# Where the padding mask is added in a cross attention of 1601 keys: TensorE's product or VectorE, tile by tile

## The reference

```python
q = _split_heads(query @ Wq.T + bq)        # 16 heads of 16 channels
k = _split_heads(key @ Wk.T + bk)
v = _split_heads(value @ Wv.T + bv)
scores = jnp.einsum('bhqd,bhkd->bhqk', q, k) / jnp.sqrt(jnp.float32(DEPTH))
scores = scores + mask * jnp.float32(-1000000000.0)
weights = jax.nn.softmax(scores, axis=-1)
ctx = jnp.einsum('bhqk,bhkd->bhqd', weights, v)
```

## Time and profile before

| | |
|---|---|
| median of 3 runs | 2710.78 us |
| lowest, highest | 2704.63, 2714.89 us |
| the profiled execution, its time | 2712.94 us |
| its span, first to last instruction | 2711.2 us |
| mean granted TensorE clock | 0.882 |
| busy: TensorE, VectorE, ScalarE, GpSimd | 2228.2, 1308.1, 956.8, 687.1 us |
| first cross attention, exp of the first to the last tile | 79.2 to 921.4 us (start of the last) |
| second cross attention, scoresT of the first to the last tile | 1439.0 to 2307.5 us |

### The profile page before, as it was taken

How to read it: one execution, slowest core, us unless ns; L and a number is a source line. 1 busy time by engine, 2 the same in 40 slices (tenths; PEclk the granted TensorE clock), 3 DMA queues, 4 the chain that set the end, 5 groups by cost and what they waited for, 6 DMA issues and landing times. The chain is left out here.

```text
span 2711.2 us, 59977 instructions
## 1 busy us (share of the span) xinstructions
PE 2228.2 (82%) x24624; PEld 1817.9 (67%) x24624; DVE 1308.1 (48%) x2900; ACT 956.8 (35%) x1689; POOL 687.1 (25%) x505
## 2 busy tenths in 40 slices
PE   5799999999999732869958999999999999844443
PEld 3677887888888611659946888888888888422223
DVE  3445454554545478231144545454545455344445
ACT  3244444444444232213232444444444444110001
POOL 3121222122121000100043443344434440033320
PEclk9799999999999675969987999999999999765557
DMA  4455555555554100143235555565565653000000
GB/s 116 112 132 127 136 128 138 124 126 136 130 130 105 44 21 0 35 144 109 79 100 131 137 141 140 137 141 139 138 143 141 142 122 79 18 0 0 0 0 22
DMA packets 166860, 267.45 MB, mean 99 GB/s; under 512 B 70713, under 2 KB 86210, under 8 KB 166594
## 3 DMA queue, kind: packets, MB, share of 16 engines
q1 hardware_dynamic: 166594, 263.66, 39.3%
HBM read 98.70 MB, written 1.05 MB: 37 GB/s over the span
## 5 line engine op out<-in xcount | busy, mean ns | idle before, releaser
L691 DVE CUSTOM_DVE_ANT_0 scores_d<-scores_d,mask_scaled_d 128x512 f32<-128x512 f32 (+1 forms) x512 | 281.4, 601 | 145.8 <-PE scores_d L536 142.8
L648 ACT ACTIVATE exp_d<-scoresT_d 128x512 f32<-128x512 f32 (+1 forms) x416 | 248.6, 598 | 274.2 <-PE scoresT_d L570 272.0
L695 DVE TENSOR_REDUCE max_parts_a<-scores_a 128x1 f32<-128x512 f32 (+1 forms) x512 | 263.6, 567 | 152.1 <-PE scores_a L536 152.1
L648 ACT ACTIVATE exp_a<-scoresT_a 128x512 f32<-128x512 f32 (+1 forms) x416 | 248.2, 597 | 210.5 <-PE scoresT_a L570 208.8
L570 PEld LDWEIGHTS scoresT_d<-q_stack_d,k_stack_d 128*128 128x128 f32 (+1 forms) x1664 | 244.8, 187 | 24.1
L570 PE MATMUL scoresT_a<-q_stack_a,k_stack_a 128*128 128x128 f32 (+1 forms) x1664 | 259.4, 281 | 0.9 <-DVE q_stack_a L712 0.9
L570 PEld LDWEIGHTS scoresT_a<-q_stack_a,k_stack_a 128*128 128x128 f32 (+1 forms) x1664 | 230.2, 195 | 28.0 <-issue 3.2
L570 PE MATMUL scoresT_d<-q_stack_d,k_stack_d 128*128 128x128 f32 (+1 forms) x1664 | 228.0, 260 | 0.0
L536 PE MATMUL scores_a<-k_stack_a,q_stack_a 96*128 96x512 f32 (+1 forms) x512 | 175.2, 395 | 42.7 <-DMA k_stack_a<-k_hi_a 20.7
L679 DVE SCALAR_TENSOR_TENSOR k_lo_d<-project_d,bk_d,k_hi_d 128x512 fp32r<-128x512 f32 (+1 forms) x128 | 81.0, 635 | 258.2 <-ACT k_hi_d L631 258.2
L679 DVE SCALAR_TENSOR_TENSOR k_lo_a<-project_a,bk_a,k_hi_a 128x512 fp32r<-128x512 f32 (+1 forms) x128 | 81.0, 635 | 253.5 <-ACT k_hi_a L631 253.4
(11 more groups left out here) (371 smaller groups left out, 4882.6 us busy)
## 6 DMA issues: line engine op xcount, KB each, us to landing
k_stack_a<-k_hi_a SPq DMA_DIRECT2D x256, 128.0 KB
k_stack_d<-k_hi_d SPq DMA_DIRECT2D x256, 128.0 KB
raw_a<-in_ctxT SPq DMA_DIRECT2D x48, 512.0 KB, 4.1
raw_d<-in_ctxT SPq DMA_DIRECT2D x48, 512.0 KB, 4.9
w_c<-in_L_ffn_W SPq DMA_DIRECT2D x23, 1024.0 KB, 8.7
k_stack_a<-k_hi_a SPq DMA_DIRECT2D x256, 72.2 KB, 2.1
k_stack_d<-k_hi_d SPq DMA_DIRECT2D x256, 72.2 KB
k_stack_a<-k_lo_a SPq DMA_DIRECT2D x128, 128.0 KB
```

The source lines that it names most:

```text
L648: nc.scalar.activation(eT[at % RING][0:r, :], ST[at % 2][0:r, :], ACT.Exp).then_inc(exp_done, 1)
L691: nc.vector.tensor_tensor_reduce(SC[at % 3][:, 0:w], SC[at % 3][:, 0:w], mf[m % 2][:, BANK * chunk:BANK * chunk + w], 1.0, NEG, ALU.add, A ...
L695: nc.vector.reduce_max(parts[:, j, chunk:chunk + 1], SC[at % 3][:, 0:w], AX.X).then_inc(score_free, 1)
```

## The change

In tiles 0, 1, 3, 7, 9 and 12 of the second attention scoresT has no mask product. VectorE adds the mask into the PSUM bank instead: scalar_tensor_tensor computes mask x -1e9 + scores over 128 x 512, the mask read from a new tile mT, laid out by keys, and repeated over the 8 heads. exp of these tiles waits for that add. In VectorE's list the add comes first in its slot. mT is a new input, transposed and cut to these six tiles on the host; one DMA a sequence brings it (196 KB), two at the start and then one behind keys(g + 2, 1) in odd iterations, where it waits for the last add of its buffer's former sequence. mb keeps only columns 256 to 1536, so GpSimd's copy and subtraction shrink from 1601 to 1280 columns. own0 goes, its two uses write into rec. The first attention is built from the same functions and keeps its instructions, but for own0.

```diff
--- before.py
+++ after.py
@@ -292,6 +292,8 @@
 S_SLOT = {0: [0], 1: [1], 2: [2, 3], 3: [4], 4: [5, 6], 5: [7], 6: [8, 9], 7: [10], 8: [11, 12], 9: [13], 10: [14, 15]}
 SUM_SLOT = 5
 MAX_SLOT = 11
+ADD_TILES = [0, 1, 3, 7, 9, 12]
+SPLIT_FROM, SPLIT_TO = 2 * P, 12 * P
 GROUPS = HALVES * NB
 
 
@@ -326,7 +328,7 @@
 PROJECTION, SCORE = projections(), score_banks()
 
 
-def cross_attention(nc, chip, cross, qT, attnT, wk, wv, bk, bv, mask, late, late_in, tag):
+def cross_attention(nc, chip, cross, qT, attnT, wk, wv, bk, bv, mask, maskT, late, late_in, tag):
 
     masked = mask is not None
     RING = 3
@@ -347,11 +349,12 @@
         qs = [sb(f"q_stack{i}", [P, PAIRS, P], F32R) for i in range(2)]
         turn, high = sb("neg_max_cols", [P, PW]), sb("neg_max_hi", [P, 4], F32R)
         parts = sb("max_parts", [P, 4, 4])
-        kept, rec, own0 = sb("out_copy", [P, P]), sb("rec", [P, P]), sb("own0", [P, T])
+        kept, rec = sb("out_copy", [P, P]), sb("rec", [P, P])
         if masked:
             mf = [sb(f"mask_scaled{i}", [P, KEYS]) for i in range(2)]
-            mb = [sb(f"mask_hi_lo{i}", [P, KPAD], F32R) for i in range(2)]
+            mb = [sb(f"mask_hi_lo{i}", [P, SPLIT_TO - SPLIT_FROM], F32R) for i in range(2)]
             pick = sb("pick", [P, P], F32R)
+            mT = [sb(f"maskT{i}", [P, len(ADD_TILES), T]) for i in range(2)]
         SC = [ctx.enter_context(nc.psum_tensor(f"scores{i}{tag}", [P, BANK], F32)) for i in range(3)]
         ST = [ctx.enter_context(nc.psum_tensor(f"scoresT{i}{tag}", [P, BANK], F32)) for i in range(2)]
         PJ = [ctx.enter_context(nc.psum_tensor(f"project{i}{tag}", [P, BANK], F32)) for i in range(2)]
@@ -360,6 +363,7 @@
         set_up, q_hi_done, q_split, q_in, q_ready = (
             sem(n) for n in ("set_up", "q_hi_done", "q_split", "q_in", "q_ready"))
         mask_in, mask_step, mask_ready = [sem(f"mask_in{i}") for i in range(2)], sem("mask_step"), sem("mask_ready")
+        maskT_in, mask_added = [sem(f"maskT_in{i}") for i in range(2)], sem("mask_added")
         k_projected, v_projected, k_hi_done = sem("k_projected"), sem("v_projected"), sem("k_hi_done")
         project_free = [sem(f"project_free{i}") for i in range(2)]
         stacked = [sem("stacked_a"), sem("stacked_b")]
@@ -413,8 +417,15 @@
                     sp.dma_start(mf[m % 2][T * k:T * k + T, :],
                                  mask[m:m + 1, :, :].rearrange("a q k -> (a q) k")).then_inc(mask_in[m % 2], 16)
 
+            def masksT(m):
+                if m >= 2:
+                    sp.wait_ge(mask_added, 2 * len(ADD_TILES) * (m - 1))
+                sp.dma_start(mT[m % 2][:, :, :], maskT[m:m + 1, :, :, :].rearrange("a p t q -> p (a t) q")
+                             ).then_inc(maskT_in[m % 2], 16)
+
             if masked:
                 masks(0)
+                masksT(0)
             queries(0)
             cross.load(sp, 1, 0)
             cross.load(sp, 1, 1)
@@ -422,6 +433,7 @@
             keys(0, 1)
             if masked:
                 masks(1)
+                masksT(1)
             queries(1)
             keys(1, 0)
             keys(1, 1)
@@ -438,6 +450,8 @@
                         queries(n + 2)
                 keys(g + 2, 0)
                 keys(g + 2, 1)
+                if masked and h and n + 2 < NB:
+                    masksT(n + 2)
             sp.wait_ge(ctx_ready, 4 * NB)
             for tile, view in late:
                 sp.dma_start(tile, view).then_inc(late_in, 16)
@@ -474,9 +488,9 @@
                 pool.wait_ge(mask_in[m % 2], 32 * (m // 2) + 32)
                 nc.gpsimd.tensor_scalar(raw[:, :], raw[:, :], -1.0e9, None, ALU.mult).then_inc(mask_step, 1)
                 pool.wait_ge(mask_step, 2 * m + 1)
-                nc.gpsimd.tensor_copy(out[:, 0:KEYS], raw[:, :]).then_inc(mask_step, 1)
+                nc.gpsimd.tensor_copy(out[:, :], raw[:, SPLIT_FROM:SPLIT_TO]).then_inc(mask_step, 1)
                 pool.wait_ge(mask_step, 2 * m + 2)
-                nc.gpsimd.tensor_tensor(out[T:P, 0:KEYS], raw[T:P, :], out[T:P, 0:KEYS].bitcast(F32),
+                nc.gpsimd.tensor_tensor(out[T:P, :], raw[T:P, SPLIT_FROM:SPLIT_TO], out[T:P, :].bitcast(F32),
                                         ALU.subtract).then_inc(mask_ready, 1)
                 pool.wait_ge(mask_ready, m + 1)
 
@@ -562,14 +576,15 @@
                     if masked and h == 0:
                         pe.wait_ge(mask_ready, m + 1)
                 after(pe, exp_done, at - 1)
-                if masked:
-                    nc.tensor.matmul(bank[0:r, :], mb[m % 2][:, cols],
+                by_product = masked and t not in ADD_TILES
+                if by_product:
+                    nc.tensor.matmul(bank[0:r, :], mb[m % 2][:, P * t - SPLIT_FROM:P * t - SPLIT_FROM + P],
                                      pick[:, :].rearrange("p (a c) -> p a c", a=1).to_broadcast([P, 4, P]),
                                      start=True, stop=False, skip_group_check=True)
                 for j in range(4):
                     ins = nc.tensor.matmul(bank[0:r, P * j:P * j + P], stack[h][:, j, cols],
-                                           qs[m % 2][:, 4 * h + j, :], start=not masked, stop=True,
-                                           skip_group_check=masked)
+                                           qs[m % 2][:, 4 * h + j, :], start=not by_product, stop=True,
+                                           skip_group_check=by_product)
                 ins.then_inc(scoredT, 1)
 
             def values(g, t):
@@ -643,7 +658,10 @@
 
             def exp(g, t):
                 at, r = KT * g + t, rows(t)
-                act.wait_ge(scoredT, at + 1)
+                if masked and t in ADD_TILES:
+                    act.wait_ge(mask_added, len(ADD_TILES) * g + ADD_TILES.index(t) + 1)
+                else:
+                    act.wait_ge(scoredT, at + 1)
                 after(act, values_done, at - RING + 1)
                 nc.scalar.activation(eT[at % RING][0:r, :], ST[at % 2][0:r, :], ACT.Exp).then_inc(exp_done, 1)
 
@@ -694,6 +712,16 @@
                 else:
                     nc.vector.reduce_max(parts[:, j, chunk:chunk + 1], SC[at % 3][:, 0:w], AX.X).then_inc(score_free, 1)
 
+            def add_mask(g, t):
+
+                at, r, m, i = KT * g + t, rows(t), g // 2, ADD_TILES.index(t)
+                if i == 0 and g % 2 == 0:
+                    dve.wait_ge(maskT_in[m % 2], 16 * (m // 2) + 16)
+                dve.wait_ge(scoredT, at + 1)
+                bank = ST[at % 2][0:r, :].rearrange("p (a q) -> p a q", q=T)
+                nc.vector.scalar_tensor_tensor(bank, mT[m % 2][0:r, i:i + 1, :].to_broadcast([r, BANK // T, T]), -1.0e9,
+                                               bank, ALU.mult, ALU.add).then_inc(mask_added, 1)
+
             def negate(g):
 
                 cols, at = turn[:, 0:16].rearrange("p (j k) -> p j k", k=4), SCORE["max", g]
@@ -724,10 +752,10 @@
                 dve.wait_ge(score_free, at + 1)
                 nc.vector.tensor_tensor(rec[:, :], kept[:, :], rec[:, :], ALU.mult).then_inc(out_step, 1)
                 dve.wait_ge(out_step, 3 * g + 1)
-                nc.vector.tensor_scalar(own0[:, :], rec[:, 0:T], own[:, 0:1], bv[:, h:h + 1], ALU.mult,
+                nc.vector.tensor_scalar(rec[:, 0:T], rec[:, 0:T], own[:, 0:1], bv[:, h:h + 1], ALU.mult,
                                         ALU.add).then_inc(out_step, 1)
                 dve.wait_ge(out_step, 3 * g + 2)
-                nc.vector.scalar_tensor_tensor(attnT[:, h, T * n:T * n + T], rec[:, T:P], own[:, 1:2], own0[:, :],
+                nc.vector.scalar_tensor_tensor(attnT[:, h, T * n:T * n + T], rec[:, T:P], own[:, 1:2], rec[:, 0:T],
                                                ALU.mult, ALU.add).then_inc(out_step, 1)
 
             nc.vector.memset(turn[:, :], 0.0)
@@ -744,6 +772,8 @@
             for g in range(GROUPS):
                 m, h = g // 2, g % 2
                 for t in range(KT):
+                    if masked and t in ADD_TILES:
+                        add_mask(g, t)
                     if t == MAX_SLOT and g + 1 < GROUPS:
                         negate(g + 1)
                         place_max(g + 1)
...
@@ -1874,6 +1904,9 @@
     a = {k: np.asarray(v) for k, v in inputs.items()}
     o = {"x": a["x"].reshape(NT, P, D), "constants": CONSTANTS, "dispatch_tables": TABLES, "ctxT": a["ctx_1024"].transpose(0, 2, 1),
          "mask": a["mask_Bx1xSxS2_fk0"].reshape(NB, T, KEYS)}
+    by_key = np.zeros((NB, KT * P, T), np.float32)
+    by_key[:, :KEYS] = o["mask"].transpose(0, 2, 1)
+    o["maskT"] = by_key.reshape(NB, KT, P, T)[:, ADD_TILES].transpose(0, 2, 1, 3)
     for k, v in a.items():
         if k.startswith(("L0_", "L1_")):
             o[k] = v
```

More of the change, by code:

```diff
@@ L1774, in _, with cross_stage @@
                                                ALU.mult, ALU.add)
-def cross_stage(nc, chip, dram, layer, tag, mask):
+def cross_stage(nc, chip, dram, layer, tag, mask, maskT):
```

(6 more changed lines are left out.)

## The result

| | before | after |
|---|---|---|
| median of 4 runs each (before: the three above and one more) | 2707.70 us | 2749.22 us |
| lowest, highest | 2695.89, 2714.89 | 2740.09, 2757.90 |
| the profiled execution | 2712.94 | 2757.90 |
| second attention, first to last instruction on its tiles | 971.1 | 1005.6 |

The ratio is 1.0157, 95% interval 1.0107 to 1.0208: the change is slower by 1.6%, outside the range forecast. A **drop** is a stretch of a few us in groups 2 to 29 in which TensorE's granted clock is 1.2 GHz; a group without one is called clean.

What follows compares the result with a forecast made beforehand. TensorE's own instructions were taken to bound the second attention. Loop -1.7, last groups +4 and start-up +1.2 gave +3.5 us on the profiled 2712.94, so 2716.4, or 2714 as median; range 2692 to 2732.

Steps and rivals of the forecast that it cites:

- clock 1.00: Expected sign in the trace after: TensorE's granted clock stays full in the second attention.
- rival B: Second attention: short idles lower TensorE's clock to 0.98, +17 us over the loop, 2731 in all; chance 0.15.
- The add: VectorE's mask add in each changed tile: 0.72 us, lower bound 0.61.
- Slots 3 to 5: Chain from tile 3's add to spread_sums: 0.69 us won, 0.66 given back, TensorE's idle there near 0.9.
- Slot 9: Odd groups: values(8) waits, leaving TensorE 0.12 us ahead; even groups: score 13 waits some 0.15, 0.34 ahead.
- Slot 12: Odd group's end: values(12) waits over 1 us for exp, group 0.77 longer; even groups covered, 0.57 shorter.
- The DMAs' waits at even groups: Score 0's waits for key stacks at even groups' starts vanish behind longer odd groups: -0.31 us a pair of groups.
- Start-up: Two new mask DMA issues ahead of the first queries and keys: +1.2 us.
- Last groups: Last two groups, without projections: 7.5 adds show at 0.53 us each, +4 us.
- A: Slots 3 to 5 have slack, only tile 12's odd-group wait is paid: -1.64 us a pair, 2691; chance 0.22.
- C: VectorE's add takes 0.95 us, deciding from over 0.9: +16 us, 2730; chance 0.13.
- D: A removed product isn't worth 0.23 us; halved, about +5, within no change; chance inside the main chain's 0.50.

Runs made afterwards that it cites:

- e12: The changed kernel with adds only in tiles 0, 1, 7 and 12, mask products back in 3 and 9: 2740.32 us, ratio 1.0105 to before.
- e1: The changed kernel with tile 12 back on TensorE's mask product, the other five adds kept: 2704.62 us, ratio 1.0007 to before.
- e4: The changed kernel with values of tile 12 issued behind the next group's scoresT(0): 2722.43 us, ratio 1.0075 to before.
- e7: The changed kernel with four thrown-away products in the wait for exp of tile 12 at odd groups' ends: 2723.15 us, ratio 1.0043 to before.
- e11: The changed kernel with thrown-away products at odd groups' ends and in the six tiles of groups 29 to 31: 2712.99 us, ratio 0.9999 to before.
- e3: The changed kernel with neither mask product nor add in the six tiles: 2702.65 us, ratio 0.9969 to before.

## Why the prediction was wrong

**The step that failed** is "clock 1.00": the sum left the clock out and held it in rival B, at chance 0.15. B's condition came true, windows under 1.00, and so did the prediction's own sign of being wrong, a granted clock that falls in the stage. The runs show its cause, the 1.26 us behind tile 12 (e12 keeps it and most drops, e1 takes it away, e4 covers half of it, e7 fills it). B's +17 for the loop was near the 18.9 that the drops cost, but it had no term for the last two groups, where the clock cost 15.4 of the 19.7 (e11, at full clock, is 4.3 over before, after is 19.7). The Trainium skill, "TensorE: Matmul & The Clock Gate", section on psum-queue depth-cycling, tells of a kernel in which frequent micro-idles between groups of matmuls make the clock swing; after agrees, with 11 drops at an idle share of 3%.

The prediction says that no row of before shows this for such idles alone. The trace of before has such rows, in the first attention, and they weren't read: its groups 2 to 29 hold 7 drops, each with a wait of 1.1 to 2.7 us for the key stack just ahead of it or at its start. One of them, and the window around it:

```profile
516.16 0.80 PE L536 MATMUL scores_a<-k_stack_a,q_stack_a 96*128 96x512 f32 x1 [1.33 <-DMA k_stack_a<-k_hi_a]
```

```profile
514.00:520.00 6.00, 4.67 (x38) 4.34 (x31) 0.69 (x1) 1.21 (x3) 2.39 (x3) 0.72 0.53 118
```

The last 61 us of that stage, same code but no mask product, showed the end ahead of time:

```profile
860.00:921.00 61.00, 57.63 (x810) 49.20 (x808) 26.30 (x55) 24.42 (x44) 0.00 (x0) 0.76 0.23 54
```

Taking masks from TensorE makes the second attention resemble this one; the prediction had the earlier trace rows's 0.98 before it and didn't ask what made it.

**Point by point.** The add: 0.72 forecast, 0.705 measured. Slots 3 to 5: the chain and its wait are as told, but the idle time is 0.53 where 0.9 was forecast; k_hi starts 0.50 after an exp listed with 0.60, two ScalarE instructions overlap, and TensorE was less far ahead. Slot 9: the step named values(8) as waiting for exp(9), but it is values(9) that needs it, later in the same run, and it doesn't wait; the 0.15 of score 13 in even groups didn't come either. Slot 12: over 1 us forecast, 1.26 measured. The DMAs' waits at even groups: gone, as said. The loop without drops: 54.86 - 0.11 = 54.75 a pair forecast, 54.46 measured in e11, with odd groups of 26.91 and even ones of 27.55 where 27.1 and 27.6 were forecast: apart from the clock the arithmetic of the waits was close, too dark by 0.29 a pair. Start-up: +1.2 forecast, +0.9 measured. Last groups: +4 forecast, +4.3 in e11 at full clock (with thrown-away products in it), +19.7 in fact. "TensorE's busy share down by 3 points": 2.3.

**Rivals.** A, -1.64 a pair, was further from the -0.40 that e11 shows for products and waits without the clock than the chosen -0.11. It would have needed a steady clock too: even e3, without any add, gains 1.23 a pair with its three drops, and 1.77 in the groups without one, where the DMAs hold score 0. C is out, the add takes 0.705. D isn't shown: e3 can't price the product by itself, since the DMAs take part of its gain back.

## What to carry to other kernels

When work leaves a saturated TensorE, look first at what its clock does where the same stream is already thinner, and give a wait like the 1.26 us here the price of a clock drop, not its own length. Thrown-away products in the gap tell in one run whether a loss is the wait's or the clock's. Before moving work away for a gain, find the next chain over the same stretch, here 12 DMA issues in one queue, since it caps what can be won.

## What the hardware showed that wasn't expected

- An idle time of 1.26 us once in about 55 us, in windows where TensorE was 97% busy, went with 11 stretches at 1.2 GHz in 14 pairs, 18.9 us in all by e11; with it taken away, halved or filled, at most one was left. At the end of the stage TensorE stayed at 1.2 GHz for 50 us while busy 48.85 of them.
- Adding four useless products a pair made the kernel 1.1% faster (1.0157 to 1.0043).
- The 12 issues of a key piece hold SP 8.4 us (median in e3) and nearly set the time from tile 7 of an odd group to the next score 0. Four of them on ScalarE's queue gave 22 us, with five drops fewer in the first attention.
